# Last two attention steps with three score banks, expert choice from turned gates, slot lists before the first expert's transpose

## The reference, cut to what it computes

```python
x = x + ga * attention(layernorm(x) * (1 + ca) + sa)     # 4 x 512 tokens, D = 128, 16 heads of 8
h = layernorm(x) * (1 + cb) + sb                          # the rows that the experts read
S = sigmoid(h @ Wg).T                                     # 8 experts x 2048 tokens
G, I = top_k(S, 512)                                      # each expert takes its 512 best tokens
hid = gelu(einsum('ekh,ehf->ekf', h[I], W1) + b1)         # FF = 512
out = (einsum('ekf,efh->ekh', hid, W2) + b2) * G[..., None]
x = x + gb * zeros.at[I].add(out)
```

## Time and profile before

| | |
|---|---|
| three runs | 436.19, 440.38, 443.81 us (median 440.38) |
| profiled execution | 442.51 us, its span 440.7 us |
| mean granted TensorE clock | 0.865 |
| busy over the span | PE 74%, DVE 64%, ACT 45%, POOL 37% |

### The profile page before, as it was taken

The page is one execution under the profiler, slowest core; times in us unless marked ns, Lnnn a source line. Parts: engine busy times, 40 slices in busy tenths (PEclk is TensorE's granted clock), DMA queues, the critical chain, the costliest instruction groups (busy, mean ns, idle before and its releaser), DMA issues.

```text
span 440.7 us, 7483 instructions
## 1 busy us (share of the span) xinstructions
PE 325.5 (74%) x2383; PEld 153.8 (35%) x2383; DVE 283.5 (64%) x569; ACT 200.4 (45%) x377; POOL 163.1 (37%) x188
## 2 busy tenths in 40 slices
PE   5699537899999999999999895310357898870940
PEld 3353103333333333333334354300224575540630
DVE  4987997798999999999967614678642324220210
ACT  2413330588888888888877520100032223220110
POOL 2607751151111111111113602100084788888672
PEclk9999957899999999999999959555586999896785
DMA  7302675011111111111005000001422565454232
GB/s 235 79 0 71 204 238 175 32 39 38 39 38 38 38 44 40 39 43 47 10 1 146 26 0 25 1 0 59 138 63 61 136 137 135 90 94 82 27 30 18
DMA packets 34344, 30.39 MB, mean 69 GB/s; under 512 B 5264, under 2 KB 28560, under 8 KB 34320
## 3 DMA queue, kind: packets, MB, share of 16 engines
q1 hardware_dynamic: 28176, 23.65, 17.3%
q0 software_dynamic: 6144, 6.43, 9.3%
HBM read 18.27 MB, written 11.60 MB: 68 GB/s over the span
## 4 chain that ended last, share of the span: by engine, by line
PE 45%; DVE 16%; POOL 15%; issue 12%; ACT 4%; DMA 3%; another core or an unknown queue 1%; SPq 0%; DVEq 0%; ACTq 0%; POOLq 0%
PE ps L1160 14%; PE ps L1123 8%; POOL out L494 8%; PE ps L1146 6%; DVE mx L787 5%; POOL ex L483 4%; PE ps L1349 3%; DVE big L901 3%; PE ps L1381 2%; PE ps L1173 2%; ACT osb L576 2%; PE ps L1247 2%; PE ps L1213 1%; DMA ex<-rows,idx 1%
## 5 line engine op out<-in xcount | busy, mean ns | idle before, releaser
L787 DVE TENSOR_REDUCE mx<-ps 128x2 f32<-128x1024 f32 x128 | 148.3, 1217 | 9.7 <-PE ps L1123 9.4
L599 ACT ACTIVATE big<-ps 128x512 f32<-128x512 f32 x256 | 139.4, 597 | 32.3 <-PE ps L1146 30.2
L1160 PE MATMUL ps<-big,VA 128*32 128x256 f32 (+1 forms) x960 | 82.0, 413 | 2.3 <-ACT osb L576 2.3
L1123 PE MATMUL ps<-KB,QB 48*128 48x512 bf16 x256 | 52.0, 405 | 12.5 <-DVE mx L787 9.8
L1146 PE MATMUL ps<-QB,KB 51*128 51x512 bf16 x256 | 55.9, 386 | 2.9 <-ACT big L599 1.3
L494 POOL DMA_INDIRECT out<-big,idx x32 | 50.6, 1582 | 14.0 <-issue 8.8
L483 POOL DMA_INDIRECT ex<-rows,idx x32 | 34.4, 1073 | 57.4 <-DVE idx L1010 43.2
L645 ACT ACTIVATE big<-ps,b1c 128x512 f32<-128x512 f32 x32 | 22.0, 687 | 63.4 <-PE ps L1349 59.0
L1349 PE MATMUL ps<-big,w1s 128*128 128x512 f32 x64 | 36.3, 687 | 2.8 <-DVE big L973 1.7
L413 POOL COPY VA<-Vall 128x128 f32 (+1 forms) x16 | 4.6, 290 | 82.8 <-PE ps L1160 82.8
L1123 PEld LDWEIGHTS ps<-KB,QB 48*128 48x128 bf16 x256 | 12.3, 93 | 58.1 <-DVE mx L787 30.8
(11 more groups left out here) (164 smaller groups left out, 419.9 us busy)
## 6 DMA issues: line engine op xcount, KB each, us to landing
KB<-k_parts SPq DMA_DIRECT2D x32, 96.0 KB
QB<-q_parts SPq DMA_DIRECT2D x32, 96.0 KB
w1s<-in_w SPq DMA_DIRECT2D x8, 256.0 KB
w2s<-in_w SPq DMA_DIRECT2D x8, 256.0 KB
k_parts<-big SPq DMA_DIRECT2D x4, 384.0 KB, 3.2
q_parts<-big SPq DMA_DIRECT2D x4, 384.0 KB, 4.1
QB<-mxp SPq DMA_DIRECT2D x96, 2.0 KB
rows<-rw SPq DMA_DIRECT2D x1, 1088.0 KB, 6.0
```

What stands on the lines that cost most here:

```text
L599: nc.scalar.activation(PT[:, u, 2 * i + half, kc, :], ps[:, banks[n], :], ACT.Exp, scale=SCALE).then_inc(s_ex, 1)
L787: nc.vector.tensor_reduce(mx[:, u, :].rearrange("p (h a) -> p h a", h=2)[:, :, n], ps[:, max_bank(u, n):max_bank(u, n) + 2, :], AX.X, ALU.max,
L1123: ins = mm(ps[:, max_bank(u, n) + half, :], QB[rows, r, i, qc * 128:(qc + 1) * 128], KB[rows, r, i, :], start=True, stop=True)
L1160: ins = mm(ps[32 * j:32 * j + 32, 6, cols], VA[:, u, kc, j, :], PT[:, u, j, kc, cols], start=kc == 0 and not cols.start, stop=kc == TC - 1 ...
```

## The change

1. Steps 14 and 15 keep the three score banks 4, 5, 7. `out_turn` of steps 12 to 15 goes to bank 2, and the transposes `turn_a` and `turn_h` share banks 0 and 3 by turns (`A_BANKS`). The work beside the score units is laid out anew, one piece per pair of units: turn_a 0, turn_a 1, project 0, turn_a 2, project 1, none, project 2; in step 15 turn_h 0, turn_h 1, gates 0, turn_h 2, gates 1, none, gates 2.
2. `route_top` and `wg_wide` go. `gates_in` runs as soon as a batch's logits are there and writes `g_en` (experts ahead of tokens); one transpose of `g_en` into bank 3 and one VectorE copy give `sv`. GpSimd copies the gates into the rows (`gates_row`), which the DMA of the rows now waits for. On GpSimd `rows_2` moves behind `values(15, 1)` and `rstd_2(2)`.
3. The 96 small matmuls of experts 2 to 7 run without a break, and expert 0's `turn` and `rows_up` come behind them and behind `idx`.

```diff
-TURN_BANKS, LAST_TURN = (0, 2), 7
+TURN_BANKS, LAST_TURN = (0, 2), 2
+A_BANKS = (0, 3)
...
             rstd_2(0)
             rstd_2(1)
-            rows_2(0)
+            values(15, 1)
             rstd_2(2)
-            values(15, 1)
-            rows_2(1)
-            rows_2(2)
+            for b in range(NB - 1):
+                rows_2(b)
+            for b in range(NB - 1):
+                gates_row(b)
             rstd_2(3)
             rows_2(3)
+            gates_row(3)
...
-            dve.wait_ge(s_sig, 1)
-            nc.vector.tensor_scalar_add(junk, sv, 1.0).then_inc(s_sig, 1)
...
-            nc.vector.reciprocal(sv, junk)
...
+            nc.vector.tensor_copy(sv, ps[:, 3, 0:128]).then_inc(s_sig, 1)
...
-            step(3, 2, more_max=False, beside=beside_14, banks=(4, 5) * 8)
+            pe.wait_ge(l_tab, 96)
+            step(3, 2, more_max=False, beside=beside_14)
...
-                if n in (0, 3, 7):
-                    turn_h(n // 3)
-                elif n in (2, 5):
-                    route_top(n // 3)
-                    route_gates(n // 3)
-                elif n == 6:
-                    out_turn(14, LAST_TURN)
+                for at, stage, b in ((0, turn_h, 0), (1, turn_h, 1), (2, route_gates, 0), (3, turn_h, 2),
+                                     (4, route_gates, 1), (6, route_gates, 2)):
+                    if n == at:
+                        stage(b)
...
+            pe.wait_ge(s_g, NB)
+            nc.tensor.transpose(ps[:, 3, 0:128], g_en[:].rearrange("p e n -> p (e n)"), ident[:]).then_inc(s_lg, 1)
...
-                    if n == 1 and e == TURN_AT:
-                        turn(0, 0)
...
+            turn(0, 0)
             up(0, 0, range(FC))
```

More of the change, by code:

```diff
@@ L582, in gates_out, with step @@
                 nc.scalar.activation(ge[:, cols], ps[:, 1, cols], ACT.Exp, scale=-1.0).then_inc(s_ge, 1)
-            def step(s, u, prev=True, more_max=True, last=False, banks=EXP_BANKS):
+            def step(s, u, prev=True, more_max=True, last=False):
                 for n in range(16):
@@ L592, in step @@
                         out_copy(14)
-                    if n in (7, 13) and last:
-                        gates_out(n // 8)
+                    if n in (7, 10, 14) and last:
+                        gates_out((7, 10, 14).index(n))
                     i, kc, half = n // 8, (n // 2) % 4, n % 2
@@ L608, in _ @@
                 step(it * 2 + 1, 1)
-            step(14, 0, banks=(4, 5) * 8)
-            step(15, 1, more_max=False, last=True, banks=(4, 5) * 8)
+            step(14, 0)
+            step(15, 1, more_max=False, last=True)
             out_copy(15)
-            gates_out(2)
-            act.wait_ge(s_lg, 1)
-            nc.scalar.activation(sv, ps[:, 3, 0:128], ACT.Exp, scale=-1.0).then_inc(s_sig, 1)
             gates_out(3)
@@ L868, in _ @@
             a_out(0)
+            a_out(1)
             residual(0)
-            a_out(1)
+            a_out(2)
             residual(1)
-            a_out(2)
+            normed(12, LAST_TURN)
             normed_2(0)
-            normed(12, LAST_TURN)
             residual(2)
@@ L879, in _ @@
             h2_out(1)
+            gates_in(0)
             normed(13, LAST_TURN)
+            h2_out(2)
+            gates_in(1)
             normed(14, LAST_TURN)
-            h2_out(2)
+            gates_in(2)
             normed(15, LAST_TURN)
@@ L1138, in exp_unit @@
                     pe.wait_ge(l_e[r], (q + 1) * 96)
-                if banks is EXP_BANKS and n == 4:
-                    pe.wait_ge(s_mn, s + 2)
-                elif banks is EXP_BANKS and n > 4:
+                if n == 4:
+                    pe.wait_ge(s_mn, min(s + 2, NS) if isinstance(s, int) else s + 2)
+                elif n > 4:
                     pe.wait_ge(s_ex, 16 * s + n - 2)
@@ L1166, in out_turn @@
                 pe.wait_ge(s_oe, s + 1)
-                if bank == LAST_TURN:
-                    pe.wait_ge(s_mn, NS)
+                if isinstance(s, int) and s >= 12:
+                    pe.wait_ge(s_mxd, 8 * NS)
                     pe.wait_ge(s_no, s)
@@ L1200, in turn_h, with route_gates @@
                 pe.wait_ge(s_xn2, b + 1)
-                if b >= 1:
-                    pe.wait_ge(s_h2e, b)
+                if b < 2:
+                    pe.wait_ge(s_aTe, 3 - b)
+                if b == 2:
+                    pe.wait_ge(s_h2e, 1)
                 for c in range(TC):
-                    ins = nc.tensor.transpose(ps[:, 2, c * 128:(c + 1) * 128], xn2[:, b % 2, c, :], ident[:])
+                    ins = nc.tensor.transpose(ps[:, A_BANKS[b % 2], c * 128:(c + 1) * 128], xn2[:, b % 2, c, :], ident[:])
                 ins.then_inc(s_h2t, 1)
-            def route_top(b):
+            def route_gates(b):
                 pe.wait_ge(s_h2e, b + 1)
-                for c in range(TC):
-                    n = b * TC + c
-                    ins = mm(ps[:, 3, 0:128], wg_wide[:, 15 - n:143 - n], h2T[:, b % 2, c * 128:(c + 1) * 128],
-                             start=n == 0, stop=n == NB * TC - 1)
-                if b == NB - 1:
-                    ins.then_inc(s_lg, 1)
-            def route_gates(b):
                 pe.wait_ge(s_x2, max(b, NB - 2) + 1)
@@ L1235, in beside_14 @@
             def beside_14(n):
-                for at, stage, b in ((0, turn_a, 0), (1, project, 0), (2, turn_a, 1), (4, project, 1),
-                                     (5, turn_a, 2), (7, project, 2)):
+                for at, stage, b in ((0, turn_a, 0), (1, turn_a, 1), (2, project, 0), (3, turn_a, 2),
+                                     (4, project, 1), (6, project, 2)):
                     if n == at:
@@ L1247, in stay_warm, with step @@
                     mm(ps[:, 6, 0:256], warm_x[:, 0:128], warm_x, start=True, stop=True)
-            def step(q, r, prev=True, prev2=True, more_max=True, turn=True, beside=None, banks=EXP_BANKS):
+            def step(q, r, prev=True, prev2=True, more_max=True, turn=True, beside=None):
                 s, u = q * 4 + r, r % 2
```

64 lines of the change are left out of this document (30 added, 34 removed).

## The result

The changed kernel takes **438.40 us** (median of 20 runs, 436.20 to 440.19), the kernel before 441.21 us in the same measurement (20 runs, 436.19 to 444.34). The ratio is **0.9951, 95% interval 0.9929 to 0.9972**: 2.2 us less (1.3 to 3.1), under half of the 5.1 us that the prediction summed. The ratio compares means without the three slowest runs of the kernel before, which lie over 1.5% above its fastest; the medians above, of all runs, lie 2.8 us apart. The profiled execution took 437.57 us with a span of 435.7 us, at a mean granted clock of 0.869; that of before took 442.51 us at 0.865, so this pair lies 4.9 us apart. Runs made later on other chips gave the same changed kernel 432.4 and 432.5 us beside 437.7 and 437.2 us for the kernel before; why, is the main subject of the experiments.

What follows compares the result with a forecast made beforehand. TensorE was taken to bound steps 14 and 15, a VectorE-TensorE-VectorE chain the token choice, GpSimd everything from the first gather. Gains 0.1 + 1.2 + 0.45 + 0.25 + 3.1 = 5.1 us, from 440.38 to 435.3 us; range 433 to 438.

Steps and rivals of the forecast that it cites:

- the term of the token numbers: Unbroken 96 small matmuls let expert 3's gather start sooner, and the gain reaches the kernel's end: 3.1 us.
- the clock in step 15: TensorE's clock falls to half in step 15 as before, so the 4.6 us loss stays and nothing is gained.
- GpSimd is the limit to expert 6's scatter: From the gathers to that scatter GpSimd sets the pace, with every expert's result ready some 3 to 5 us early.
- Step 14: TensorE through some 0.7 us sooner, not passed on because out_copy(13) comes later: gain 0.1 us, taken as nothing.
- Step 15: Less TensorE work as three route_tops leave, half the saving eaten by a wait: gain 1.2 us at equal clock.
- full-clock walk of the kernel before: Old step 15's TensorE work summed at full clock: 7.8 us from 252.41, ending at 260.2.
- new wait: Step 15: TensorE waits 1.2 us before turn_h(2), as GpSimd's moved rows_2 collides with VectorE's normed_2(2).
- Rival A: The clock holds through step 15: 432.8 us, down to 429.8; range 429.5 to 433.5, chance 0.30.
- Entry to the rounds: From batch 3's gates to the first count: 3.51 us in place of 3.96, gain 0.45 us.
- Rounds: Gate work leaves rounds 10 to 13, about 0.06 us each: gain 0.25 us, bounds 0 and 2.0.
- Rival B: Token numbers gain 1.4 us or less, with up(0) all at half clock: 437 us, range 437 to 439, chance 0.10.
- Rival C: Slower: the wait at turn_h(2) drops the clock, which stays low behind step 15: 442 us, range 440 to 445, chance 0.07.

Runs made afterwards that it cites:

- again: The changed kernel itself, unchanged, timed and traced anew: 432.43 us, ratio 0.9867 to the kernel before.
- again2: The changed kernel itself, unchanged, timed and traced once more: 432.54 us, ratio 0.9902 to the kernel before.
- p3_only: The kernel before with only part 3 of the change (96 small matmuls unbroken, expert 0's turn and rows_up behind them): 435.21 us, ratio 0.9965.
- two_bank: The changed kernel with two score banks (4 and 5) instead of three in steps 14 and 15: 433.26 us, ratio 0.9887.
- rows2: The changed kernel with GpSimd's rows_2(0) back ahead of values(15, 1) and rstd_2(2): 432.77 us, ratio 0.9863.
- twice: The changed kernel with the 96 small matmuls issued twice, 192 in one run beside the gathers: 431.8 us.
- no_p3_b: Second run of the changed kernel with part 3 undone (expert 0's turn again ahead of the 49th small matmul): 433.69 us, ratio 0.9919.
- before_b: The kernel before, unchanged, in a third trace: 434.82 us.
- before_a: The kernel before, unchanged, in a second trace: 436.03 us.
- eight: The changed kernel with the 96 small matmuls issued eight times, 768 in one run beside the gathers: 449.5 us.
- flood: The changed kernel with three extra 1 MB memory-to-memory copies of x beside the gathers and the 96 small matmuls: 439.2 us.
- flood8: The changed kernel with 768 small matmuls in one run and three extra 1 MB copies of x beside them: 454.8 us.
- flood8_b: The same kernel as flood8, run once more: 455.4 us, ratio 1.0317.

## Why the prediction was right or wrong

**The sum was too large in the recorded measurement, and where it came out right, it did so by luck.** Forecast 5.1 us; between the medians 5.2 (again) and 4.7 (again2), by the ratios 5.8 and 4.3, and on record 2.8 between the medians and 2.2 by the ratio. Two steps failed: the term of the token numbers, 3.1 us with "I let the gain reach the end", and the clock in step 15, which was forecast to fall in the change as before and so stood in the sum as nothing. The condition named at its end came true: "if TensorE's issue stalls for more than 3 us in the 96 matmuls"; 4.7 us are listed, 7.3 with what follows.

| us | forecast | before and after, profiled | traces without a stall or a fall |
|---|---|---|---|
| steps 14 and 15 at equal clock | 1.3 | 1.6 | 1.6 |
| clock in step 15 | 0 | 4.6 | 0 |
| entry and rounds | 0.7 | 0.55 | 0.55 |
| first gather to the end | 3.1 | -1.5 | 0.8 |
| sum | 5.1 | 5.0 (spans; 0.25 lost ahead of step 14) | 2.9 |

In the profiled pair 4.6 us of clock hide a miss of 4.6 us in the token numbers. On the chips without a stall the equal-clock terms give 2.9 us, not the measured 4.3 to 5.8; the clock's fall makes up the rest as an estimate, since it cost the old step 15 1.9 us on the mean of four traces (4.6, 3.1, 0, 0) and the new one 0.1 on the mean of sixteen. Four traces are few for a mean. With the token numbers at -1.5 the same estimate gives 2.4 for the recorded measurement, near the 2.2 of the ratio.

**Token numbers, forecast 3.1.** The place of expert 3's gather was right: 23.0 - 3.1 = 19.9 us after the first was forecast, and the six traces without a stall that have part 3 and no padding or delay (p3_only, again, again2, two_bank, rows2, and twice with 19.87) give 19.2 to 20.2. Two sizes were off. First, the 23.0 subtracted from held a stall itself: four traces without part 3 on other chips have 20.6 to 21.9, so the true gain there is about 1.5 us. Secondly, the gain did not reach the end: from the first gather to the end it is 117.6 to 118.2 without and 116.0 to 117.8 with part 3, some 0.8 us on average, in line with the 1.15 us between again2 and no_p3_b. At expert 5's scatter the mean gain is still 1.45 us; at expert 6's it is 0.9. There GpSimd finds expert 6's result late in four of the six, as in again (and in one of the four without part 3), and waits 2.0 us for an earlier scatter in the two others, as in again2 (first row again, second again2):

```profile
407.76 1.55 POOL L498 DMA_INDIRECT out<-big,idx  x1 [3.25 <-DVE big L1025]
407.65 1.55 POOL L498 DMA_INDIRECT out<-big,idx  x1 [1.97 <-DMA out<-big,idx]
```

So "GpSimd is the limit to expert 6's scatter", with every result ready some 3 to 5 us early, was wrong at that scatter. In the recorded traces the sign turned. Against the stall-free traces, after lost about 5.2 us from the first gather to the end (122.2 against a mean of 117.0), before 2.8 (120.7 against 117.9).

That every one of the 20 recorded runs stalled is argued, not shown: their lowest, 436.2 us, lies above the highest of the 12 later runs of the same code, 433.6.

**Step 14, forecast 0.1:** measured to the first weigh of step 15, as the prediction did, a loss of 0.2 us (from oc(12) 241.35 - 226.74 = 14.61 before, 241.80 - 226.99 = 14.81 after). TensorE being through sooner was not passed on, as said; out_copy(13) came a little later still than the 240.6 I gave it.

**Step 15, forecast 1.2 at equal clock:** from the first weigh to oc(15) it is 261.41 - 242.53 = 18.88 us in p3_only and 258.92 - 241.80 = 17.12 in after, a gain of 1.76. Both steps gain 33.49 - 31.93 = 1.56 us, against 1.3 forecast. The full-clock walk of the kernel before (260.2) was right too: before_b needs 20.15 us from oc(13), the walk 260.2 - 240.08 = 20.1. The new wait is real but cost 0.3 us (rows2), not 1.2: TensorE arrived at 249.0 and not 248.4, and normed_2(2) was done some 0.3 us sooner than said.

**The clock:** forecast to fall as before; it held. Rival A, at 0.30, should have been the main case for step 15. It didn't bring rival A's time (432.8): the profiled execution lies 4.8 us above it, since the token numbers took their 4.6 us back. And the loss of 4.6 us was no property of the kernel before: it comes in some executions. The sentence of the Trainium skill that the prediction weighed ("HAM oscillation — how this bites in real kernels") puts falls down to long idle gaps. before_a falls behind gaps of 0.69 us at most, so the traces still contradict it here, and before_b, with the same gaps and no fall, shows that neither the rule nor a row of one profile decides it.

**Entry to the rounds, forecast 0.45:** 0.14 from the gates' start to the first count (the gates took 1.88 us, not 1.75), 0.31 from oc(15). Single traces of either kernel lie between 14.8 and 15.9 here: in again2, with 15.85, the clock was at half from 263 to 266 us, so 0.31 holds for a like clock only. **Rounds, forecast 0.25:** 39.88 to 39.64, 0.24. The rows' DMA and GpSimd's copies had cover, as said.

**Rival B** (token numbers gain less) came true in its direction, and even in its time (437, profiled 437.57), for another reason than up(0)'s clock. **Rival C** (slower) had little support: the clock fell behind the wait in one trace of sixteen (again), and was back within 3 us.

## What to carry to other kernels

Take a second trace before pricing a loss that one trace shows: the clock's fall in step 15 and the stall at the end of the 48 matmuls were both in the profile that the prediction subtracted from; the first was missing in one of the next two traces, the second in both. A sum that comes out right can hide two terms that are wrong by the same amount, so compare it stage by stage. A long run of tiny matmuls depends on TensorE's supply of instructions, which gave out after some 70 of them beside the gathers on some chips; whether a turn or a wait in their midst covers that was not tested on such a chip (the kernel before had one there and still stalled, behind 42 of its second 48). Where an engine idles 2 us ahead of work that waits for data, and its clock halves just then, two useless matmuls in the gap and the order of rows2 were together worth some 3 us (429.4 against 432.5). By the traces 0.34 us of it is the order's and 0.9 to 2.3 the matmuls' (first gather to the end 115.5 us, against 116.4 in again2 and 117.8 in rows2).

## What the runs showed of the hardware

TensorE's instruction supply can be the limit. No trace shows the fetch itself; it is read from the idle time put down to issue, and from gaps that come after every 256 instructions in eight. Where it was plentiful, 128x32 matmuls ran at 0.026 us each for 342 in a row, then in lots of 128 in 3.35 us with 0.39 to 0.66 us between. Where it was short, 67 to 71 ran at that rate, then mostly 4 to 6 every 0.73 us with some pauses of 1.1 us, for 7.7 to 8.0 us up to the next work of the chain (after, flood, flood8, flood8_b). In flood8 the bursts end at 327.7 us, 1.3 us behind GpSimd's last gather instruction (325.42 + 0.95), and the same execution then runs 494 matmuls at once; this points to the gathers' traffic as one condition. The same traffic did nothing to the 342 of eight, so there is a second. Left open: what it is, and whether the chip sets it. By the few runs there are, the kernel before took 440 to 442 us where stalls came and medians of 434 to 438 where they did not.

The collision of VectorE and GpSimd on small instructions repeats closely between executions: four of normed_2 take 1.11 us alone, 2.89 to 2.91 beside two of GpSimd's in the four traces with the old order (2.68 in rows2), and 4.18 beside three in after, again and again2.
